# A cross-attention and mixture-of-experts kernel: the loads of x behind the first pair wait for that pair, and Wq is transposed ahead of the first rows

## The chip, the cores and the metric

The kernel runs on one core of a Trainium2 chip. Its engines are TensorE (PE), VectorE (DVE), ScalarE (ACT), GpSimd (POOL) and SyncE (SP); each works through its own list of instructions in order and waits on semaphores. The metric is the device time of one execution in microseconds, as the median of several runs.

## The reference

All arrays are float32. x is 8 blocks of 128 tokens with 256 features, the context 8 blocks of 128 rows with 64.

```python
x = x + xattn(layernorm(x), ctx, Wq, Wkv, Wout)   # causal, 16 heads of 16, within each block
x = x + ffn(layernorm(x), ...)                    # 8 experts, the best 2 of a token, LoRA of rank 16

# xattn(q, latent_kv)
qp = q @ Wq.T
k, v = split(latent_kv @ Wkv.T)
attn = softmax(where(causal, qh @ kh.T * 0.25, min))
out = (attn @ vh) @ Wout.T
# ffn
logits = x @ (gate_weight + 2 * gate_lora_B @ gate_lora_A).T
weights of the top 2 of softmax(logits), divided by their sum
gup = x @ gate_up_proj[e] + 2 * lora;  h = silu(gates) * up
y = sum over the chosen e of weight * (h @ down_proj[e] + 2 * lora)
```

## The kernel before

The order of every engine is written out by hand. The 8 blocks of tokens are handled in pairs (p = 0 to 3) up to the projections, one by one in attention, and in two groups of four in the feed-forward part, where for each of 16 (group, expert) steps TensorE multiplies in float32r with split high and low parts.

The start concerns us. What happens to pair p of x:

- SP loads it into `x_sb` (line 191, semaphore `x{p}`); the four pairs are 256 KB each. Behind them stand on SP's queue the LoRA B loads (lines 194 and 195, in runs of 64 bytes), Wout (196), the LoRA A loads (199, 200), and then, for each block, the maxima of its scores (`load_max`, line 205), which are moved into rows of `q_f` before the transposed scores of that block.
- VectorE takes its statistics (`pair_stats`, lines 540 and 541), GpSimd makes rstd (`normaliser`, lines 253 and 254), VectorE normalises into `xhat` (`normalise_pair`, line 553).
- TensorE transposes xhat into a bank (`x_T`, line 833), and ScalarE copies that to `xT` (`input_copy`, line 318).
- TensorE projects: `k_proj` (line 851) needs only the context's transpose `cT` and Wkv; `q_proj` (line 804 with `wq_d`) needs `xT` and the transposed, scaled Wq. ScalarE and VectorE spread the results into `k_f` and `q_f` (lines 345 and 565).

The other inputs of the start come on ScalarE's queue (lines 320 to 324), in this order: Wkv, the first half of the context, Wq (256 KB), the second half of the context, and half of `up_w` (1 MB). GpSimd issues the other half of `up_w` (line 270) and `dn_w` (line 273) between its normalisers. Wq is transposed by four instructions (line 1109) into bank 2, and ScalarE copies them to `wq_d` (`wq_copy`, line 318).

VectorE's program begins with `pair_stats(0)`, `wkv_dup(0)`, `normalise_pair(0)`, `context_dup(0)`, `pair_stats(1)`, `k_copy(0)`, `normalise_pair(1)`, `q_copy(0)`, `wkv_dup(1)`, `context_dup(1)`, `pair_stats(2)`, `normalise_pair(2)` and then the four `max_chunk`s of block 0 (line 594). Of these, `pair_stats(1)` waits for the load of the second pair, and everything behind it in the list waits with it. TensorE transposes the maxima of block 0 (`max_T`, line 944) after its second q and k projections, and goes on to the scores of block 1.

Of the kernel before, what the change touches and what calls it, by code (L numbers as in the profile page):

```python
# [12 lines left out]
def cross_attention_moe_kernel(nc, x, ctx_kv, Wq, Wkv, Wout, gate_w, gate_A, gate_B,  # L13
# [16 lines left out]
    PN = 2 * P  # L30
# [18 lines left out]
    with ctx:  # L49
# [38 lines left out]
        first = sb("first", [P, 2])  # L88
# [99 lines left out]
        @block.sync  # L188
        def _(sp):
            for p in range(NP):  # L190
                sp.dma_start(x_sb[:, 2 * p:2 * p + 2, :], x_v[:, 2 * p:2 * p + 2, :]).then_inc(ld[f"x{p}"], 16)
            sp.wait_ge(S_("pads_zero"), 2)
            for c in range(HC):
                sp.dma_start(upB[:, c, :, 0:R], gup_B.rearrange("e (c p) r -> c p e r", p=P)[c]).then_inc(ld["upB"], 16)
                sp.dma_start(dnB[:, c, :, 0:R], down_B.rearrange("e (c p) r -> c p e r", p=P)[c]).then_inc(ld["dnB"], 16)
            sp.dma_start(wo_raw[:, :, :], Wout.rearrange("(c p) h -> p c h", p=P)).then_inc(ld["wo"], 16)
            for j in range(4):
                rows = slice(32 * j, 32 * j + R)
                sp.dma_start(upA[rows, :, :], gup_A.rearrange("(k j) r h -> j r k h", j=4)[j]).then_inc(ld["upA"], 16)
# [12 lines left out]
            for b in range(1, NT):  # L212
                load_max(b)

            for g in range(NG):

                sp.wait_ge(S_("wT_copied"), g + 1)
                sp.dma_start(w_dram[g], wT[:, g, :]).then_inc(S_("w_written"), 16)
                sp.wait_ge(S_("w_written"), 16 * (g + 1))
                for i in range(E):  # L220
                    if g == 0:
                        sp.wait_ge(S_("pv_done"), NT - 1 if i < E // 2 else NT)
                    else:
# [92 lines left out]
        def _(act):  # L316
# [30 lines left out]
            def k_copy(p):  # L347
                act.wait_ge(S_("k_proj_0"), p + 1)
                for u in range(2):
                    spread(k_f[:, 2 * u, pair(p)], K_BANK(p, 0)[:, 0:PN], u, first[:, 1 - u:2 - u], "k_by_act")  # L350

            def q_copy(p):
                act.wait_ge(S_("q_proj_0"), p + 1)
                for u in range(2):
                    spread(q_f[:, 2 * u, pair(p)], Q_BANK(p, 0)[:, 0:PN], u, zero_col[:, :], "q_by_act")

            def values(g):
                act.wait_ge(S_("v_ones"), 1)
# [70 lines left out]

            wkv_copy(0)  # L430
            context_copy(0)
            input_copy(0)
            wq_copy()
            act.wait_ge(S_("masks_made"), 1)
            k_copy(0)
            q_copy(0)
# [90 lines left out]
        def _(dve):  # L527
# [39 lines left out]
            def k_copy(p):  # L567
                dve.wait_ge(S_("k_proj_1"), p + 1)
                for u in range(2):
                    spread(k_f[:, 2 * u + 1, pair(p)], K_BANK(p, 1)[:, 0:PN], u, first[:, 1 - u:2 - u], "k_by_dve")  # L570

            def q_copy(p):
                dve.wait_ge(S_("q_proj_1"), p + 1)
                for u in range(2):
                    spread(q_f[:, 2 * u + 1, pair(p)], Q_BANK(p, 1)[:, 0:PN], u, zero_col[:, :], "q_by_dve")

            def merge(n):

# [221 lines left out]
        def _(pe):  # L800
# [14 lines left out]
            def context_T(p):  # L815
                pe.wait_ge(ld[f"ctx{p // 2}"], 16)
                if p in (1, 2):
                    pe.wait_ge(S_("k_by_dve"), 2 * p)
                if p == 3:
                    pe.wait_ge(S_("o_nat_ready"), 1)  # L820
                for t in range(2):
# [3 lines left out]
            def x_T(p):  # L825
                pe.wait_ge(S_("xhat_ready"), 2 * (p + 1))
                if p in (1, 2):
                    pe.wait_ge(S_("k_by_act"), 2 * p)
                if p == 3:
                    pe.wait_ge(S_("merged"), 6)  # L830
                for ic in range(HC):
# [22 lines left out]
            def q_proj(p):  # L854
# [1 line left out]
                if p == 0:  # L856
                    pe.wait_ge(S_("wq_ready"), 1)
                if p == 1:
                    pe.wait_ge(S_("q_by_act"), 2)
                    pe.wait_ge(S_("q_by_dve"), 2)  # L860
                if p == 2:
                    pe.wait_ge(S_("v_ready"), 2)
                    pe.wait_ge(S_("mT_copied"), 2)
# [8 lines left out]
            def v_proj(g):  # L872
                pe.wait_ge(S_("wkv_dup"), 2)
                pe.wait_ge(S_("cT_dup"), 2 * (g + 1))
                if g == 0:
                    pe.wait_ge(S_("q_by_act"), 4)
                    pe.wait_ge(S_("q_by_dve"), 4)
                    pe.wait_ge(S_("mT_copied"), 1)
                else:
                    pe.wait_ge(S_("oT_copied"), 4)  # L880
# [9 lines left out]
            def scores(s, s_js, t, t_js):  # L890

                if s is not None:
                    if s_js[0] == 0 and s % 2 == 0:
                        for by in ("q_by_act", "q_by_dve", "k_by_act", "k_by_dve"):
                            pe.wait_ge(S_(by), 2 * (s // 2 + 1))
                    for j in s_js:
                        n = NC * s + j
# [28 lines left out]
            def max_T(b):  # L926
                pe.wait_ge(S_("max_done"), NC * (b + 1))
                if b == 0:
                    pe.wait_ge(S_("q_by_act"), 4)
                if b == 1:  # L930
                    pe.wait_ge(S_("v_ready"), 2)
                if b in (2, 3):
                    pe.wait_ge(S_("merged"), 3 * (b - 2) + 2)
                if b == 4:
                    pe.wait_ge(S_("q_by_dve"), 8)
                if b == 5:
                    pe.wait_ge(S_("k_by_dve"), 8)
                if b == 6:
                    pe.wait_ge(S_("v_ready"), 4)
                if b == 7:  # L940
# [73 lines left out]
            def values(b):  # L1014
# [2 lines left out]
                if b < 2:  # L1017
                    pe.wait_ge(S_("merged"), 3 * b + 1)
                if b == 2:
                    pe.wait_ge(S_("q_by_act"), 8)  # L1020
                if b == 3:
                    pe.wait_ge(S_("k_by_act"), 8)
                if b > GT:
                    pe.wait_ge(S_("merged"), 2 * b - 3)
                if b:
# [76 lines left out]
            pe.wait_ge(ld["wkv"], 16)  # L1102
            wkv_T(0)
            context_T(0)
            x_T(0)
            pe.wait_ge(ld["wq"], 16)
            for ic in range(HC):
                for oc in range(HC):
                    last = pe.transpose(bank[2][:, ic * H + oc * P:ic * H + (oc + 1) * P],
                                        wq_raw[:, oc, ic * P:(ic + 1) * P], ident[:, :])  # L1110
            last.then_inc(S_("wq_T"), 1)
            k_proj(0)
            q_proj(0)
            wkv_T(1)
# [14 lines left out]
            for b in range(NT):  # L1129
# [8 lines left out]
                if b == 1:  # L1138
# [1 line left out]
                    pe.wait_ge(S_("merged"), 3)  # L1140
                    pe.transpose(bank[7][0:R, 0:E], gb_raw[:, :], ident[0:E, 0:E]).then_inc(S_("gb_T"), 1)
                    pe.wait_ge(ld["wo"], 16)
                    pe.wait_ge(S_("k_by_dve"), 6)
                    for ic in range(HC):
                        for oc in range(HC):
                            last = pe.transpose(bank[5][:, ic * H + oc * P:ic * H + (oc + 1) * P],
# [19 lines left out]
                if b == 0:  # L1166
                    pe.wait_ge(ld["upA"], 64)
                    pe.wait_ge(ld["dnA"], 64)
                    pe.wait_ge(S_("k_by_act"), 6)
                    pe.wait_ge(S_("q_by_act"), 6)  # L1170
                    pe.wait_ge(S_("q_by_dve"), 6)
                    lora_products(range(3))
                if b == 1:
                    pe.wait_ge(S_("oT_copied"), 1)
# [77 lines left out]
```

## Time and profile before

| | us |
|---|---|
| median of 3 runs | 166.98 (166.35 to 167.42) |
| the profiled execution | 165.62 |
| its span | 163.9 |

| engine | busy us | share of the span |
|---|---|---|
| TensorE | 151.0 | 92% |
| VectorE | 105.4 | 64% |
| ScalarE | 80.1 | 49% |
| GpSimd | 53.7 | 33% |

The span runs from the first to the last instruction that the profiler records; the execution's own time is 1.72 us more. The page's chain is followed back from the last instruction: at each step to what released it. Transfers are busy in two stretches early on (the inputs, up to 24 us) and later around the expert weights of the tokens and the stores.

### The profile page before, as it was taken

To read this page: it belongs to the slowest core of one execution; us is meant where nothing else is said; L and a number is where in the kernel's file an instruction comes from. 1 tells how busy PE (TensorE), PEld (TensorE's weight loads), DVE (VectorE), ACT (ScalarE), POOL (GpSimd) and SP (SyncE) were. 2 spreads that over 40 slices of the span, in tenths; PEclk is the share of its full clock that TensorE was granted. 3 is DMA by queue.
4 is the path that set the end of the run, shared out by engine and by line. 5 is a ranking of instruction groups with operands and counts; after the bars stand their busy time and mean duration, and the time that the engine had idled before them with its cause. 6 is when DMAs were issued, how large, how long until landed. Compare 5 with 4: busy or idle time off the path is not lost.

```text
span 163.9 us, 3777 instructions
## 1 busy us (share of the span) xinstructions
PE 151.0 (92%) x1481; PEld 119.7 (73%) x1481; DVE 105.4 (64%) x224; ACT 80.1 (49%) x161; POOL 53.7 (33%) x93
## 2 busy tenths in 40 slices
PE   0598599999999999999999999999999999999991
PEld 0275366676786677777887887888888888888991
DVE  2757887695957664884459835884696348744443
ACT  1364247654675757766676452664463222222230
POOL 5271401245638575777773124351000000000000
PEclk9999999999999999999999999999999999999999
DMA  5999960000000000000000017600000873000003
GB/s 130 308 263 200 258 213 0 2 7 5 4 4 1 3 6 4 2 4 2 4 0 0 4 42 244 231 4 0 2 0 15 224 278 130 0 0 0 4 0 128
DMA packets 13041, 11.18 MB, mean 68 GB/s; under 512 B 6456, under 2 KB 10448, under 8 KB 13024
## 3 DMA queue, kind: packets, MB, share of 16 engines
q1 hardware_dynamic: 9584, 7.14, 16.4%
q0 software_dynamic: 544, 2.10, 4.5%
q10 hardware_dynamic: 2896, 1.70, 4.1%
q8 instruction: 12, 0.20, 0.5%
q14 instruction: 5, 0.04, 0.1%
HBM read 9.79 MB, written 1.08 MB: 66 GB/s over the span
## 4 chain that ended last, share of the span: by engine, by line
PE 77%; DVE 13%; issue 2%; DMA 2%; ACT 2%; POOL 1%; DVEq 0%; ACTq 0%
PE bank L804 37%; PE bank L1093 11%; PE bank L914 7%; DVE m_sb L594 4%; PE bank L1030 4%; PE bank L900 4%; PE bank L921 3%; DMA x_sb<-in_x 2%; PE bank L979 2%; DVE xhat L553 2%; PE bank L1011 1%; PE bank L833 1%; PE bank L885 1%; PE bank L990 1%; DVE up_w L587 1%
## 5 line engine op out<-in xcount | busy, mean ns | idle before, releaser
L295 POOL TENSOR_SCALAR_AFFINE_SELECT probsT<-probsT 128x512 f32<-128x512 f32 x32 | 19.8, 638 | 21.3 <-ACT probsT L391 21.3
L391 ACT ACTIVATE probsT<-bank 128x512 f32<-128x512 f32 x32 | 18.0, 590 | 17.3 <-PE bank L921 17.3
L804 PE MATMUL bank<-xT_hi,up_hi 128*128 128x512 f32 x64 | 26.1, 407 | 0.0
L594 DVE TENSOR_REDUCE m_sb<-bank 128x4 f32<-128x512 f32 x32 | 20.4, 683 | 8.7 <-PE bank L914 8.7
L804 PE MATMUL bank<-xT_hi,up_lo 128*128 128x512 f32 x64 | 25.3, 395 | 0.0
L804 PE MATMUL bank<-xT_lo,up_hi 128*128 128x512 f32 x64 | 25.3, 395 | 0.0
L318 ACT ACTIVATE h_hi<-h_f 128x512 fp32r<-128x512 f32 x16 | 10.1, 631 | 29.9 <-PE bank L1093 24.9
L677 DVE TENSOR_TENSOR h_lo<-h_f,h_hi 128x512 fp32r<-128x512 f32 x16 | 12.5, 780 | 10.1 <-ACT h_hi L318 10.1
L921 PE MATMUL bank<-q_f,k_f 32*128 32x128 f32 x256 | 18.6, 283 | 0.0
L1093 PE MATMUL bank<-dn_hi,h_hi 128*128 128x256 f32 x64 | 18.2, 285 | 0.1
L1093 PE MATMUL bank<-dn_hi,h_lo 128*128 128x256 f32 x64 | 17.9, 279 | 0.0
L1093 PE MATMUL bank<-dn_lo,h_hi 128*128 128x256 f32 x64 | 17.8, 279 | 0.0
L914 PEld LDWEIGHTS bank<-k_f,q_f 32*128 32x128 f32 x256 | 13.6, 186 | 5.5 <-issue 5.5
L914 PE MATMUL bank<-k_f,q_f 32*128 32x128 f32 x256 | 16.3, 283 | 0.0
L921 PEld LDWEIGHTS bank<-q_f,k_f 32*128 32x128 f32 x256 | 15.5, 186 | 0.7 <-issue 0.7
L672 DVE TENSOR_TENSOR h_f<-probsT,gated 128x512 f32<-128x512 f32 x16 | 11.1, 696 | 6.2 <-DMA probsT<-weights 5.9
L804 PEld LDWEIGHTS bank<-xT_hi,up_lo 128*128 128x128 f32 x64 | 12.0, 188 | 2.9
L804 PEld LDWEIGHTS bank<-xT_hi,up_hi 128*128 128x128 f32 x64 | 12.0, 188 | 2.2
L804 PEld LDWEIGHTS bank<-xT_lo,up_hi 128*128 128x128 f32 x64 | 12.0, 188 | 2.2
L286 POOL TENSOR_TENSOR up_lo<-up_w,up_hi 128x512 fp32r<-128x512 f32 x8 | 10.2, 1277 | 9.8 <-ACT up_hi L318 9.8
L665 DVE TENSOR_TENSOR gated<-bank,silu 128x512 f32<-128x512 f32 x16 | 11.0, 688 | 3.2 <-issue 2.1
L1093 PEld LDWEIGHTS bank<-dn_hi,h_hi 128*128 128x128 f32 x64 | 12.0, 187 | 0.9 <-DVE h_lo L677 0.3
(137 smaller groups left out, 284.8 us busy)
## 6 DMA issues: line engine op xcount, KB each, us to landing
probsT<-weights SPq DMA_DIRECT2D x16, 256.0 KB, 5.3
x_sb<-in_x SPq DMA_DIRECT2D x4, 256.0 KB, 4.4
up_w<-in_L_ffn_gate_up_proj ACTq DMA_DIRECT2D x1, 1024.0 KB, 10.3
up_w<-in_L_ffn_gate_up_proj POOLq DMA_DIRECT2D x1, 1024.0 KB, 7.4
dn_w<-in_L_ffn_down_proj POOLq DMA_DIRECT2D x1, 1024.0 KB, 7.1
out<-x_sb SPq DMA_DIRECT2D x4, 256.0 KB, 2.2
ctx_sb<-in_ctx ACTq DMA_DIRECT2D x2, 128.0 KB, 5.6
wq_raw<-in_L_xattn_Wq ACTq DMA_DIRECT2D x1, 256.0 KB, 5.5
```

Of the source, the lines that this page charges most:

```text
L286: pool.tensor_tensor(merge_slice(up_lo, dn_lo, n), merge_slice(up_w, dn_w, n), merge_slice(up_hi, dn_hi, n).bitcast(F32), ALU.subtract).th ...
L295: pool.affine_select(out=ch, in_=ch, compare_op=ALU.is_ge, fill=0.0, base=0, pattern=[[0, 4], [1, P]], channel_multiplier=-1).then_inc(S_( ...
L318: act.activation(out_, in_, ACT.Copy, scale=scale).then_inc(S_(done), 1)
L391: act.activation(probsT[:, b % 2, 4 * j:4 * j + 4, :].rearrange("p h n -> p (h n)"), bank[2 + j % 2][:, :], ACT.Exp).then_inc(S_("exp_done ...
L594: dve.reduce_max(m_sb[:, b % 2, :].rearrange("p (u j t) -> p j u t", u=2, t=2)[:, c], S_BANK(b, c)[:, :].rearrange("p (u t n) -> p u t n", ...
L665: dve.tensor_tensor(gated[:, k, :], bank[2 + k][:, :], silu[:, k, :], ALU.mult).then_inc(S_("gated_ready"), 1)
L672: dve.tensor_tensor(h_f[:, k, :], weight_all[:, n % E, :], gated[:, k, :], ALU.mult).then_inc(S_("h_ready"), 1)
L677: dve.tensor_tensor(h_lo[:, k, :], h_f[:, k, :], h_hi[:, k, :].bitcast(F32), ALU.subtract)\
L804: last = pe.matmul(out_, a, m, start=start and i == 0, stop=stop and i == len(pairs) - 1, **kw)
L914: last = pe.matmul(S_BANK(s, j)[:, c * P:(c + 1) * P], q_f[rows, c, tokens(s)], k_f[rows, c, tokens(s)], start=False, stop=True, skip_grou ...
L921: last = pe.matmul(bank[2 + j % 2][:, c * P:(c + 1) * P], k_f[rows, c, tokens(t)], q_f[rows, c, tokens(t)], start=True, stop=True)
L1093: last = pe.matmul(bank[6 + t // 2][:, (t % 2) * H:(t % 2 + 1) * H], a[:, k, tok], w[:, e, :], start=i == 0 and t % 2 == 0 and m == 0, sto ...
```

## The change

SP issues the first pair of x as before, and then waits until it has landed before it issues the other three; the rest of its queue follows. On TensorE the wait for Wq and its four transposes stand ahead of the four transposes of the first pair's xhat, and ScalarE's two copies are exchanged in the same way. In addition four semaphores are renamed (`k_by_act` to `k_copied_0`, `k_by_dve` to `k_copied_1`, and the same for q), with no effect on what waits for what. The line numbers of what follows move by one or two.

```diff
@@ sync queue @@
             for p in range(NP):
+                if p == 1:
+                    sp.wait_ge(ld["x0"], 16)
                 sp.dma_start(x_sb[:, 2 * p:2 * p + 2, :], x_v[:, 2 * p:2 * p + 2, :]).then_inc(ld[f"x{p}"], 16)
             sp.wait_ge(S_("pads_zero"), 2)
@@ ScalarE, start of its program @@
             wkv_copy(0)
             context_copy(0)
+            wq_copy()
             input_copy(0)
-            wq_copy()
             act.wait_ge(S_("masks_made"), 1)
             k_copy(0)
@@ TensorE, start of its program @@
             wkv_T(0)
             context_T(0)
-            x_T(0)
             pe.wait_ge(ld["wq"], 16)
             for ic in range(HC):
                 for oc in range(HC):
                     last = pe.transpose(bank[2][:, ic * H + oc * P:ic * H + (oc + 1) * P],
                                         wq_raw[:, oc, ic * P:(ic + 1) * P], ident[:, :])
             last.then_inc(S_("wq_T"), 1)
+            x_T(0)
             k_proj(0)
             q_proj(0)
```

On TensorE, at the start of its program, before (the tile written, then the tiles read; x4 is four in a row; `wq_raw` is Wq as loaded):

```order
L812 MATMUL bank<-ident,wkv_raw 64x128 x2
L822 MATMUL bank<-ident,ctx_sb 64x128 x2
L833 MATMUL bank<-ident,xhat 128x128 x4
L1109 MATMUL bank<-ident,wq_raw 128x128 x4
L851 MATMUL bank<-cT,wkv_d 128x256 x2
L804 MATMUL bank<-xT,wq_d 128x256 x4
L812 MATMUL bank<-ident,wkv_raw 64x128 x2
```

And with the change:

```order
L814 MATMUL bank<-ident,wkv_raw 64x128 x2
L824 MATMUL bank<-ident,ctx_sb 64x128 x2
L1110 MATMUL bank<-ident,wq_raw 128x128 x4
L835 MATMUL bank<-ident,xhat 128x128 x4
L853 MATMUL bank<-cT,wkv_d 128x256 x2
L806 MATMUL bank<-xT,wq_d 128x256 x4
L814 MATMUL bank<-ident,wkv_raw 64x128 x2
```

The four transposes of Wq have moved ahead of the four that read xhat, directly behind those of the context; what follows is in the same order. On ScalarE, behind its five DMA issues and the load of its table, before:

```order
L318 ACTIVATE wkv_d<-bank 64x256
L318 ACTIVATE cT<-bank 64x256
L318 ACTIVATE xT<-bank 128x512
L318 ACTIVATE wq_d<-bank 128x512
L345 ACTIVATE k_f<-bank,first,mine 128x256 x2
L345 ACTIVATE q_f<-bank,zero_col,mine 128x256 x2
```

And with the change:

```order
L320 ACTIVATE wkv_d<-bank 64x256
L320 ACTIVATE cT<-bank 64x256
L320 ACTIVATE wq_d<-bank 128x512
L320 ACTIVATE xT<-bank 128x512
L347 ACTIVATE k_f<-bank,first,mine 128x256 x2
L347 ACTIVATE q_f<-bank,zero_col,mine 128x256 x2
```

The copy to `wq_d` stands ahead of the copy to `xT`. On SP, whose waits are shown in brackets, before:

```order
L191 DMA x_sb<-in_x 128x2x256 x4
L194 DMA upB<-in_L_ffn_gup_lora_B 128x8x16 [waits pads_zero]
L195 DMA dnB<-in_L_ffn_down_lora_B 128x8x16
L194 DMA upB<-in_L_ffn_gup_lora_B 128x8x16
L195 DMA dnB<-in_L_ffn_down_lora_B 128x8x16
```

And with the change:

```order
L193 DMA x_sb<-in_x 128x2x256
L193 DMA x_sb<-in_x 128x2x256 [waits ld_x0]
L193 DMA x_sb<-in_x 128x2x256 x2
L196 DMA upB<-in_L_ffn_gup_lora_B 128x8x16 [waits pads_zero]
L197 DMA dnB<-in_L_ffn_down_lora_B 128x8x16
L196 DMA upB<-in_L_ffn_gup_lora_B 128x8x16
```

The second load of x now waits for the semaphore of the first, and what stands behind it in the list comes after that wait.

## Rows read from the trace of the kernel before

**Rows 1.** The page: busy us (share of the span) xinstructions; then the chain's shares.
```profile
PE 151.0 (92%) x1481; PEld 119.7 (73%) x1481; DVE 105.4 (64%) x224; ACT 80.1 (49%) x161; POOL 53.7 (33%) x93
...
PE 77%; DVE 13%; issue 2%; DMA 2%; ACT 2%; POOL 1%; DVEq 0%; ACTq 0%
```

**Rows 2.** Chain of waits, 0 to 33 us: start us, us, what.
```profile
0.79 3.29 DMA x_sb<-in_x
...
6.59 0.75 DVE xhat L553 x2
...
7.38 1.11 PE bank L833 x4
8.49 0.85 PE bank L1109 x4
9.35 1.16 PE bank L851 x4
10.50 2.09 PE bank L804 x8
...
17.95 2.40 DVE m_sb L594 x4
```

**Rows 3.** Timeline of TensorE: start us, us, engine, instructions [idle before <-releaser].
```profile
5.88 0.64 PE L822 MATMUL bank<-ident,ctx_sb 128*64 128x128 f32 x2 [0.65 <-DMA ctx_sb<-in_ctx]
...
12.65 0.60 PE L833 MATMUL bank<-ident,xhat 128*128 128x128 f32 x4
...
20.39 0.28 PE L944 MATMUL bank<-ident,m_sb 128*16 128x128 f32 x1 [1.71 <-DVE m_sb L594]
...
25.90 0.38 PE L921 MATMUL bank<-q_f,k_f 32*128 32x128 f32 x2
```

**Rows 4.** Timeline of VectorE, 4 to 18 us.
```profile
7.36 0.29 DVE L562 COPY cT<-cT 64x256 f32<-64x256 f32 x1
7.68 0.43 DVE L540 BATCH_NORM_STATS2 stats<-x_sb 128x6 f32<-128x256 f32 x1
...
10.58 0.99 DVE L565 TENSOR_SCALAR k_f<-bank,mine,first 128x256 f32<-128x256 f32 x2 [1.73 <-PE bank L851]
11.49 1.00 DVE L553 TENSOR_SCALAR xhat<-x_sb,mv,rstd 128x256 f32<-128x256 f32 x2
```

**Rows 5.** Timeline of GpSimd, 2 to 18 us.
```profile
9.25 0.72 POOL L254 TENSOR_TENSOR rstd<-var_eps,minus_half 128x2 f32<-128x2 f32 x1
...
16.92 0.93 POOL L273 DMA_DIRECT2D dn_w<-in_L_ffn_down_proj  x1
```

**Rows 6.** Timeline of ScalarE and its DMA issues, 0 to 14 us.
```profile
1.87 0.53 ACTq L322 DMA_DIRECT2D wq_raw<-in_L_xattn_Wq  x1
...
8.53 0.60 ACT L318 ACTIVATE xT<-bank 128x512 f32<-128x512 f32 x1 [1.60 <-PE bank L833]
```

**Rows 7.** Tile x_sb, 0 to 26 us: issues (ns min/median/max, first and last start), time to landing.
```profile
L191 SPq DMA_DIRECT2D x_sb<-in_x x4: 433/458/472, 0.8 to 2.3; - x4
...
DMA to landing us min/median/max: 3.3/4.4/6.2
```

**Rows 8.** DMA issues: queue, KB each, us to landing.
```profile
dn_w<-in_L_ffn_down_proj POOLq DMA_DIRECT2D x1, 1024.0 KB, 7.1
out<-x_sb SPq DMA_DIRECT2D x4, 256.0 KB, 2.2
...
wq_raw<-in_L_xattn_Wq ACTq DMA_DIRECT2D x1, 256.0 KB, 5.5
wo_raw<-in_L_xattn_Wout SPq DMA_DIRECT2D x1, 256.0 KB, 7.8
```

**Rows 9.** Windows: span, engines busy (xinstructions), granted clock, DMA share, GB/s.
```profile
7.40:10.80 3.40, 3.40 (x13) 2.42 (x14) 1.57 (x6) 1.40 (x3) 1.63 (x4) 1.00 1.25 262
```

**Rows 10.** Timeline of SP's issues, 11 to 75 us.
```profile
16.22 0.42 SPq L200 DMA_DIRECT2D dnA<-in_L_ffn_down_lora_A  x1
21.00 1.26 SPq L205 DMA_DIRECT2D q_f<-mT  x2
```

More of the change, by code:

```diff
@@ L349, in k_copy @@
                 for u in range(2):
-                    spread(k_f[:, 2 * u, pair(p)], K_BANK(p, 0)[:, 0:PN], u, first[:, 1 - u:2 - u], "k_by_act")
+                    spread(k_f[:, 2 * u, pair(p)], K_BANK(p, 0)[:, 0:PN], u, first[:, 1 - u:2 - u], "k_copied_0")
             def q_copy(p):
@@ L354, in q_copy @@
                 for u in range(2):
-                    spread(q_f[:, 2 * u, pair(p)], Q_BANK(p, 0)[:, 0:PN], u, zero_col[:, :], "q_by_act")
+                    spread(q_f[:, 2 * u, pair(p)], Q_BANK(p, 0)[:, 0:PN], u, zero_col[:, :], "q_copied_0")
             def values(g):
@@ L569, in k_copy @@
                 for u in range(2):
-                    spread(k_f[:, 2 * u + 1, pair(p)], K_BANK(p, 1)[:, 0:PN], u, first[:, 1 - u:2 - u], "k_by_dve")
+                    spread(k_f[:, 2 * u + 1, pair(p)], K_BANK(p, 1)[:, 0:PN], u, first[:, 1 - u:2 - u], "k_copied_1")
             def q_copy(p):
@@ L574, in q_copy @@
                 for u in range(2):
-                    spread(q_f[:, 2 * u + 1, pair(p)], Q_BANK(p, 1)[:, 0:PN], u, zero_col[:, :], "q_by_dve")
+                    spread(q_f[:, 2 * u + 1, pair(p)], Q_BANK(p, 1)[:, 0:PN], u, zero_col[:, :], "q_copied_1")
             def merge(n):
@@ L817, in context_T @@
                 if p in (1, 2):
-                    pe.wait_ge(S_("k_by_dve"), 2 * p)
+                    pe.wait_ge(S_("k_copied_1"), 2 * p)
                 if p == 3:
@@ L827, in x_T @@
                 if p in (1, 2):
-                    pe.wait_ge(S_("k_by_act"), 2 * p)
+                    pe.wait_ge(S_("k_copied_0"), 2 * p)
                 if p == 3:
@@ L858, in q_proj @@
                 if p == 1:
-                    pe.wait_ge(S_("q_by_act"), 2)
-                    pe.wait_ge(S_("q_by_dve"), 2)
+                    pe.wait_ge(S_("q_copied_0"), 2)
+                    pe.wait_ge(S_("q_copied_1"), 2)
                 if p == 2:
@@ L875, in v_proj @@
                 if g == 0:
-                    pe.wait_ge(S_("q_by_act"), 4)
-                    pe.wait_ge(S_("q_by_dve"), 4)
+                    pe.wait_ge(S_("q_copied_0"), 4)
+                    pe.wait_ge(S_("q_copied_1"), 4)
                     pe.wait_ge(S_("mT_copied"), 1)
@@ L893, in scores @@
                     if s_js[0] == 0 and s % 2 == 0:
-                        for by in ("q_by_act", "q_by_dve", "k_by_act", "k_by_dve"):
+                        for by in ("q_copied_0", "q_copied_1", "k_copied_0", "k_copied_1"):
                             pe.wait_ge(S_(by), 2 * (s // 2 + 1))
@@ L928, in max_T @@
                 if b == 0:
-                    pe.wait_ge(S_("q_by_act"), 4)
+                    pe.wait_ge(S_("q_copied_0"), 4)
                 if b == 1:
@@ L934, in max_T @@
                 if b == 4:
-                    pe.wait_ge(S_("q_by_dve"), 8)
+                    pe.wait_ge(S_("q_copied_1"), 8)
                 if b == 5:
-                    pe.wait_ge(S_("k_by_dve"), 8)
+                    pe.wait_ge(S_("k_copied_1"), 8)
                 if b == 6:
@@ L1019, in values @@
                 if b == 2:
-                    pe.wait_ge(S_("q_by_act"), 8)
+                    pe.wait_ge(S_("q_copied_0"), 8)
                 if b == 3:
-                    pe.wait_ge(S_("k_by_act"), 8)
+                    pe.wait_ge(S_("k_copied_0"), 8)
                 if b > GT:
@@ L1142, in _ @@
                     pe.wait_ge(ld["wo"], 16)
-                    pe.wait_ge(S_("k_by_dve"), 6)
+                    pe.wait_ge(S_("k_copied_1"), 6)
                     for ic in range(HC):
@@ L1168, in _ @@
                     pe.wait_ge(ld["dnA"], 64)
-                    pe.wait_ge(S_("k_by_act"), 6)
-                    pe.wait_ge(S_("q_by_act"), 6)
-                    pe.wait_ge(S_("q_by_dve"), 6)
+                    pe.wait_ge(S_("k_copied_0"), 6)
+                    pe.wait_ge(S_("q_copied_0"), 6)
+                    pe.wait_ge(S_("q_copied_1"), 6)
                     lora_products(range(3))
```

## The prediction

> **What bounds the kernel now.** I read four views in this order. The page's busy shares and its chain come first [rows 1]: TensorE is busy for 92% of the span and makes 77% of the chain that ended last, VectorE another 13%. So the end moves when TensorE's work starts sooner or later, or when a gap in it opens or closes. The change touches only the start, so the second view is the chain in order of time there [rows 2]. The reader should see five links: the first pair of x lands at 0.79 + 3.29 = 4.08 us; statistics and normalising end at 7.34 (6.59 + 0.75); then TensorE runs without a break through four transposes of xhat (1.11), four of Wq (0.85), the k projection (1.16) and the q projection (2.09); VectorE's chain follows down to the first maxima, 17.95 to 20.35; and TensorE is released at 20.39 after 1.71 idle [rows 3]. From there it is nearly always busy. The third view is each engine's timeline beside this path [rows 3 to 6], for what is queued behind what. The fourth is the landing of transfers [rows 7, 8].
>
> The point that matters: the four transposes of Wq stand on the path between xhat and the k projection, though they need nothing from xhat. Before 7.38 TensorE has been waiting: its context transposes end at 5.88 + 0.64 = 6.52 and xhat comes 0.86 later. Wq itself was issued at 1.87 and took 5.5 [rows 6, 8], so it landed at about 7.37, exactly when xhat was ready. In the order of before it cost nothing that Wq came so late; moved forward alone, it would find its tile only at 7.37.
>
> **Part 1: Wq ahead of the first rows.** Nothing is added: four transposes and one ScalarE copy (0.60) trade places with four transposes of xhat and their copy (0.60). If Wq is in by 6.5, its transposes run from about 6.55. They took 0.85 in the chain; started alone, as those of xhat at 7.38 were, the four need up to 1.11 to the end of the last, so they are over at 7.4 to 7.7, and TensorE's input side is free at 7.4. The xhat transposes go at 7.38 as before, and end at 8.49. ScalarE copies Wq before 8.3 and xT at 8.53 as before [rows 6], done at 9.13. The k projection needs nothing more than the copies of cT (VectorE, 7.36 + 0.29 [rows 4]) and so starts 0.85 sooner, at 8.5. The q projection follows 1.16 later, at 9.65, by when xT (9.13) is there: also 0.85 sooner. VectorE's k copy moves from 10.58 to 9.73 and ends at 10.72, and the normalising of the second pair, which stands behind it in VectorE's queue, goes from 11.49 to 10.64 if its rstd is there; rstd was ready at 9.25 + 0.72 = 9.97 [rows 5]. So 0.85 reaches the second xT, the q copies, the third pair and the first maxima. **Gain 0.85.**
>
> The bounds of this term: the transposes here run slowly. Four of xhat take 1.11 at 7.38 and 0.60 at 12.65 [rows 2, 3], a ratio of 1.85, although the granted clock is given as 1.00 in this stretch too [rows 9]; I read the durations as the lower of the two clock levels until shortly after 10.5, and the upper one after. If TensorE speeds up at the same instant as before (about 10.8) while the q projection starts 0.85 sooner, then 0.85 of it runs slowly that did not: a loss of 0.85 x (1 - 1/1.85) = 0.39, and 0.46 is left. If it speeds up sooner, the gain grows (first rival). I take 0.85, since the busy stretch that came before the rise starts sooner by about as much.
>
> **Part 2: the loads held.** x1, x2 and x3 no longer stand behind x0 in SP's queue from 0.8 to 2.3, but are issued from about 4.15. Three things follow.
> - x0 itself: did the later pairs slow it? The four were issued 0.5 apart and took from 3.3 (the first) to 6.2 (the last) [rows 7], that is they landed from 4.08 to about 8.5, 1.5 apart on average: one after another, not together. So x0 was hardly shared with x1, and I take 0. The upper bound is the store of the same 256 KB at the end, 2.2 with little else moving [rows 8]: 1.1 less. The lower bound is 0; one transfer less ahead of or beside x0 can't delay it.
> - ScalarE's queue has the engines to itself from about 3.5 to 5.2. Traffic runs at 262 GB/s from 7.4 to 10.8 [rows 9]; I take that rate for the stretch before too, which x1 and x2 shared. At their spacing of 1.5 some 256 KB or more of them moved between x0's landing and Wq's last bytes; at 262 GB/s that is 1.0 us of transfer. So ctx0 (5.88 before [rows 3]) should land about 0.6 sooner and Wq about 1 us sooner, at 6.1 to 6.5. Bounds: 7.37 (nothing gained) down to 4.1 (2.2 after its issue, as the store). What it costs if this fails: with Wq at 7.37, its transposes run first, those of xhat 0.85 later, and the k projection starts at 9.35 as before; xT is copied by 9.98, still before 10.50. So part 1 then gains nothing and loses nothing.
> - x1 is late. Its statistics started at 7.68 behind the cT copy that ended at 7.65 [rows 4], so it had 2.4 us to spare. Issued at 4.15 it lands at 7.45 with x0's 3.3 (the nearest row: same size, same queue, empty before it), at 6.35 with the store's 2.2, and at 10.35 with x3's 6.2. I take 7.45: no cost. The slack beyond it: from the start of statistics to rstd is 9.97 - 7.68 = 2.29, and normalising can start at 10.64, so x1 may land as late as 8.25 before any of the 0.85 is lost, and up to 9.1 before the kernel is slower than it was.
>
> The Trainium skill (DMA: Bandwidth & Descriptors, Two DMAs through the same engine are not ordered) says that descriptors of one queue on one engine start in order. By that rule, the trace agrees: holding x1 buys x0 nothing, and speaks against the hold as a help for x0. The same page (Anatomy of one DMA) gives a fit of 2.0 us plus bytes over 436 GB/s, measured on another issuing path; an estimate by it puts x1 at 4.15 + 2.6 = 6.75, and the sum would not change.
>
> **What queues behind the held loads.** SP issues the small LoRA loads, Wout, the LoRA A loads and then the maxima of the first block behind the x loads, some 2 us later at first. Their first readers on TensorE come after 24 us, and none of the landings named in the rows is later than 24.0 (dn_w: 16.92 + 7.1 [rows 5, 8]). The tightest is the maxima: issued at 21.00 [rows 10], read by the transposed scores at 25.90 [rows 3]. They will be issued at 20.15 and read at 25.05; SP's last load before them was issued by 16.64 [rows 10], so 2 us of delay there fit. Taken at 0. The bound is Wout's 7.8 [rows 8]: with it they land at 27.95, 2.9 late.
>
> **Sum.** The profiled execution took 165.62 (span 163.9 and 1.72 around it). 165.62 - 0.85 + 0 + 0 = 164.77. The median of the three runs shown is 1.36 above that execution; by medians the forecast is 166.98 - 0.85 = **166.1**. After 20.39 I find nothing that would give the gain back: what TensorE waits for later is VectorE and ScalarE, which shift with it.
>
> **Rivals.**
> 1. TensorE speeds up earlier (chance 0.15). Wq's transposes fill the time before 7.38, so TensorE works nearly without a break from about 5. If the xhat transposes run at 0.60 instead of 1.11 and the k projection at 1.16/1.85 = 0.63, another 1.04 is there; but rstd of the second pair (9.97) caps it: normalising can go from 11.49 to 10.0 at best, so 1.49 in all, and 165.5. For it: the same instruction is 1.85 times faster once TensorE has been busy. Against: only transposes are added before 7.38. The Trainium skill (TensorE: Matmul & The Clock Gate, Part 4: PE-mode transpose) holds that transposes don't count as activity for the clock; no row here shows it, and by it this rival would not come about.
> 2. x0 sooner (0.05): up to 1.1 on top of 0.85, but SP, VectorE and GpSimd then wait for Wq or for x1; I price it at half, 165.6 to 165.0.
> 3. Nothing moves (0.09): Wq lands no earlier than 7.37, because the traffic of ScalarE's own queue, not x, sets it. 167.0.
> 4. Slower (0.09): x1 is late. One mechanism: SP's held loads come back into full traffic (ctx1 and 1 MB of up_w already queued by ScalarE) and take x3's 6.2 or even Wout's 7.8. VectorE waits at the statistics of the second pair, with the k copy behind them. Landing at 10.35 costs 10.35 - 9.1 = 1.25: 168.2; landing at 11.95 costs 2.85: 169.8. It decides from 9.1 on. Against: x0's own 3.3 was reached with ScalarE's queue beside it.
>
> **How the numbers follow.** The likeliest case has 0.62 and 166.1, its own range 165.4 to 166.8 from its bounds of 0.46 and about 1.2 and the spread of the runs shown (166.35 to 167.42). With rivals 1 to 3 and a part of 4 the range that should hold 8 in 10 is 164.9 to 167.3. About 1%, 1.67 us, is what a measurement of this kernel can tell from no change. Faster than 165.3: a part of rival 1, most of 2 and the edge of the first case, 0.20. Slower than 168.65: the later half of rival 4 and the unforeseen, 0.06. Within 1%: 0.74.
>
> **What would show it.** In the new profile: x0 still lands at 4.0 to 4.1; Wq's transposes start before 6.8 and end before xhat's start at 7.4; the k projection starts near 8.5, normalising of the second pair near 10.6, the first maxima near 17.0; and TensorE's release by the maxima's transpose falls at about 19.5. x1's landing shows in whether VectorE sits idle before 7.7's statistics. The prediction is wrong if that wait ends after 8.3, if Wq's transposes still start at 7.4, or if the xhat transposes take 0.6 instead of 1.1.

## The result, and the profile after

| | before | after |
|---|---|---|
| median, us | 166.66 (6 runs, 165.65 to 167.51) | 168.50 (6 runs, 168.03 to 169.19) |
| the profiled execution | 165.62 | 168.08 |
| its span | 163.9 | 166.3 |

The changed kernel takes 1.0115 times as long, 95% interval 1.0084 to 1.0147: 1.8 us slower, where 0.85 less was forecast. (The ratio is estimated from all single times; it is not the quotient of the two medians, which in this document differs from it by up to 0.0024.) It came out by rival 4, x1 late, to which I had given 0.09.

The page's busy line and its chain, which answer [rows 1]:

```profile
PE 153.4 (92%) x1470; PEld 121.4 (73%) x1481; DVE 105.6 (63%) x224; ACT 80.0 (48%) x161; POOL 53.3 (32%) x93
...
PE 72%; DVE 14%; DMA 6%; issue 3%; ACT 2%; POOL 1%; DVEq 0%; ACTq 0%
```

TensorE has lost share of the chain, and transfers have gone from 2% to 6%. The chain of waits at the start (start us, us, what) says which one, against [rows 2]:

```profile
0.79 3.21 DMA x_sb<-in_x
...
4.02 7.23 DMA x_sb<-in_x
...
20.39 2.40 DVE m_sb L596 x4
...
22.83 0.28 PE bank L946
```

The load of the second pair now stands on the path for 7.23 us, where it didn't appear before. The four transposes of Wq and the k projection have left the chain. TensorE's timeline shows that this part went as forecast, up to the q projection:

```profile
6.00 1.11 PE L1110 MATMUL bank<-ident,wq_raw 128*128 128x128 f32 x4 [0.28 <-DMA wq_raw<-in_L_xattn_Wq]
...
7.23 1.11 PE L835 MATMUL bank<-ident,xhat 128*128 128x128 f32 x4
...
8.27 1.23 PE L853 MATMUL bank<-cT,wkv_d 64*128 64x256 f32 x4
...
9.43 3.78 PE L806 MATMUL bank<-xT,wq_d 128*128 128x256 f32 x8
...
15.04 0.66 PE L835 MATMUL bank<-ident,xhat 128*128 128x128 f32 x4 [1.62 <-DVE xhat L555]
```

Wq's transposes start at 6.00, those of xhat at 7.23, the k projection at 8.27. Then the second xhat transposes wait 1.62 for VectorE, and the maxima's transpose comes at 22.83 instead of 20.39 [rows 3]: 2.44 later, as much as the span is longer. VectorE's timeline has the reason, against [rows 4]:

```profile
11.28 0.43 DVE L542 BATCH_NORM_STATS2 stats<-x_sb 128x6 f32<-128x256 f32 x1 [3.79 <-DMA x_sb<-in_x]
...
12.37 0.96 DVE L567 TENSOR_SCALAR k_f<-bank,mine,first 128x256 f32<-128x256 f32 x2
13.61 1.38 DVE L555 TENSOR_SCALAR xhat<-x_sb,mv,rstd 128x256 f32<-128x256 f32 x2 [0.28 <-POOL rstd L256]
```

It sits idle for 3.79 us at the statistics of the second pair, with the k copy behind them. SP issued the three held loads at once when x0 was in, 4.02 to 5.63, and the tile's landings say 7.2 for x1 (the least of the three; the 3.2 is x0's) and 7.9 for the last:

```profile
L193 SPq DMA_DIRECT2D x_sb<-in_x x4: 379/450/667, 0.8 to 5.2; - x4
...
DMA to landing us min/median/max: 3.2/7.4/7.9
```

Why so long? The queues' traffic from 4 to 8 us, first before, then after (queue: packets, MB, share of 16 engines; q1 is SP's, q10 ScalarE's):

```profile
q1 hardware_dynamic: 1059, 0.71, 63.6%
q10 hardware_dynamic: 1328, 0.55, 53.0%
```

```profile
q10 hardware_dynamic: 1802, 1.24, 107.3%
```

Before, the two queues shared the engines. After, SP's queue has no row in that stretch: it moved nothing from 4.02, when the first of the held loads was issued, to 8. From 8 to 11 it moves 0.77 MB:

```profile
q1 hardware_dynamic: 1081, 0.77, 86.0%
```

So x1 was not slowed by sharing; it had to wait until ScalarE's queue, with the second half of the context and 1 MB of up_w already in it, had nearly run out: 1.24 MB of it went from 4 to 8, and the last 0.25 MB beside SP's loads from 8 to 11. The rates show that no bandwidth was missing, 311 GB/s from 4 to 8 (314 before), and one more thing (span, engines busy, granted clock, DMA share, GB/s):

```profile
4.00:8.00 4.00, 2.97 (x12) 1.79 (x12) 2.44 (x8) 2.15 (x4) 0.95 (x2) 1.00 1.07 311
...
16.00:20.00 4.00, 3.75 (x37) 2.31 (x38) 2.33 (x8) 0.59 (x2) 1.70 (x4) 0.57 0.86 255
```

TensorE's granted clock was 0.57 on average from 16 to 20, that is mostly the lower of its two levels, after TensorE had been idle for the most part from 13.4 to 15.0. Before it was 1.00 there.

### The profile page after: what moved, and what is told of

It reads as the page before. It is cut to its first block, busy times and chain, and to the rows that moved or that the text cites. A ratio compares the mean times of both kernels' runs of the same rounds, so it can differ in the third digit from the quotient of the medians.

```text
span 166.3 us, 3766 instructions
## 1 busy us (share of the span) xinstructions
PE 153.4 (92%) x1470; PEld 121.4 (73%) x1481; DVE 105.6 (63%) x224; ACT 80.0 (48%) x161; POOL 53.3 (32%) x93
## 4 chain that ended last, share of the span: by engine, by line
PE 72%; DVE 14%; DMA 6%; issue 3%; ACT 2%; POOL 1%; DVEq 0%; ACTq 0%
PE bank L806 36%; PE bank L1095 11%; PE bank L916 7%; DMA x_sb<-in_x 6%; DVE m_sb L596 4%; PE bank L1032 4%; PE bank L923 3%; PE bank L902 3%; DVE xhat L555 2%; PE bank L981 2%; PE bank L1013 1%; PE bank L887 1%; PE bank L992 1%; DVE up_w L589 1%; DVE stats L542 1%
## 5 line engine op out<-in xcount | busy, mean ns | idle before, releaser
L916 PEld LDWEIGHTS bank<-k_f,q_f 32*128 32x128 f32 x256 | 14.4, 203 | 5.9 <-issue 5.9
L916 PE MATMUL bank<-k_f,q_f 32*128 32x128 f32 x256 | 17.2, 302 | 0.0
```

The costliest lines, as they stand in the source:

```text
L916: last = pe.matmul(S_BANK(s, j)[:, c * P:(c + 1) * P], q_f[rows, c, tokens(s)], k_f[rows, c, tokens(s)], start=False, stop=True, skip_grou ...
```

## The experiments

Theory H: the held loads are served only when ScalarE's backlog is through, and VectorE's wait for x1 is the whole loss. Rival S: the new order on TensorE costs by itself. Rival C: the lower clock is a good part of the loss. Ratios are against the kernel before on the same chip, and the three values in the column "before" are three chips. Each kernel ran 12 times, but "hold from x2, spare transposes" only 6 times at first, and the ratios of "hold only" and "TensorE kept busy" rest on 9 times each.

| kernel | median, us | before | ratio (95%) |
|---|---|---|---|
| exchange only | 167.01 | 166.34 | 1.0045 (1.0015 to 1.0075) |
| hold only | 168.14 | 166.34 | 1.0097 (1.0062 to 1.0132) |
| both, up_w late | 165.85 | 166.34 | 0.9950 (0.9921 to 0.9980) |
| both, hold from x2 | 165.74 | 166.34 | 0.9952 (0.9928 to 0.9976) |
| both, TensorE kept busy | 168.22 | 166.91 | 1.0085 (1.0051 to 1.0119) |
| hold from x2, no exchange | 166.54 | 166.91 | 0.9986 (0.9959 to 1.0013) |
| exchange, Wq on SP's queue | 165.97 | 166.91 | 0.9940 (0.9912 to 0.9967) |
| hold from x2, spare transposes | 165.21 | 166.91 | 0.9885 (0.9844 to 0.9926) |
| the same again | 166.05 | 166.59 | 0.9948 (0.9916 to 0.9980) |
| hold from x2, again | 166.15 | 166.59 | 0.9957 (0.9927 to 0.9988) |
| hold from x2, spare products | 165.91 | 166.59 | 0.9935 (0.9898 to 0.9972) |
| Wq on SP's queue, spare products | 165.44 | 166.59 | 0.9925 (0.9890 to 0.9960) |

### Each part alone

Exchange only: the change without these two lines.

```diff
-                if p == 1:
-                    sp.wait_ge(ld["x0"], 16)
```

> Only the exchange of the Wq transposes with the xhat transposes; the four x loads are issued in a row as before. Theory H (the held loads are served only when ScalarE's backlog is through, and VectorE's wait for x1 is the whole loss): x1 lands at 5.3 as before, VectorE has no wait at the statistics of the second pair, Wq lands at about 7.4, its transposes start at 7.4 and the exchange moves nothing: 166.7, within 0.5. Rival S (the new order itself costs, by the wait for Wq ahead of the xhat transposes, or through TensorE's clock): 167.5 to 168.5.

It was 0.45% slower, which neither theory had said: less than S, and not H's nothing. Its times fall in two groups, seven from 166.34 to 167.09 and five from 167.92 to 168.26, and the profiled one, at 167.98, is of the slower five. TensorE's timeline shows why that one was slow:

```profile
7.21 0.63 PE L822 MATMUL bank<-ident,ctx_sb 128*64 128x128 f32 x2 [1.85 <-DMA ctx_sb<-in_ctx]
8.83 1.11 PE L1108 MATMUL bank<-ident,wq_raw 128*128 128x128 f32 x4 [0.98 <-DMA wq_raw<-in_L_xattn_Wq]
9.73 1.06 PE L833 MATMUL bank<-ident,xhat 128*128 128x128 f32 x4
10.72 1.23 PE L851 MATMUL bank<-cT,wkv_d 64*128 64x256 f32 x4
```

In this execution the context came at 7.21 and Wq at 8.83, 1.4 later than in the profile of before. VectorE had made xhat by 7.45 (6.71 + 0.74), and its transposes stood behind Wq's until 9.73; the k projection started at 10.72, 1.44 later than before. As an estimate from these rows, 0.99 of it (from 9.73 to 10.72) is the order's, since the old one would have had the xhat transposes done while it waited for Wq; the other 0.45 is the late Wq's own. So the order is not free of risk: it puts whatever Wq is late by on the path of xhat. That a late Wq is what sets the other four slow executions apart is likely, but only one was profiled.

Hold only: the two lines alone, in the kernel before.

```diff
+                if p == 1:
+                    sp.wait_ge(ld["x0"], 16)
```

> Only the hold; TensorE and ScalarE keep the order of before. H: x1 lands at about 11.2, the second pair's normalising starts at about 13.6, time 168.5 within 0.5, the same as with both parts, since the k projection 0.85 earlier buys nothing while VectorE waits. S: 166.7, since without the exchange there is no loss.

Ratio 1.0097, on H's side, and against S; the 1.0115 of both parts can't be told from it, as the intervals overlap. VectorE's row for the second pair's statistics, and the maxima's transpose on TensorE:

```profile
10.45 0.43 DVE L542 BATCH_NORM_STATS2 stats<-x_sb 128x6 f32<-128x256 f32 x1 [3.09 <-DMA x_sb<-in_x]
```

```profile
22.00 0.28 PE L946 MATMUL bank<-ident,m_sb 128*16 128x128 f32 x1 [1.89 <-DVE m_sb L596]
```

x1 lands 0.8 earlier here than with both parts and the maxima's transpose comes 0.8 earlier too: 22.00 against 22.83, and 20.39 before.

### Is it ScalarE's backlog?

Both parts of the change, and up_w issued later:

```diff
-            act.dma_start(up_w[:, 0, :, :], gate_up.rearrange("e (c p) o -> c p e o", p=P)[0]).then_inc(ld["up0"], 16)
...
             k_copy(0)
             q_copy(0)
+            act.dma_start(up_w[:, 0, :, :], gate_up.rearrange("e (c p) o -> c p e o", p=P)[0]).then_inc(ld["up0"], 16)
             wkv_copy(1)
```

> Both parts of the change, and ScalarE issues its 1 MB of up_w behind its first q copies (about 12.6) instead of at 2.95. H: x1 finds ScalarE's queue empty once the second half of the context is through (about 6.3) and lands at 7.0 to 7.8; the statistics start at 7.7, and part 1's 0.85 shows at last: 165.8 (165.3 to 166.3). If the long latency of x1 is not made by that backlog, x1 still lands after 10 and the time stays at 168.5. S: 168 or more.

165.85, as H said: taking 1 MB out of ScalarE's queue turned 1.0115 into 0.9950, 0.8 us less than before by the ratio (0.5 by the two medians). VectorE's statistics of the second pair and its normalising:

```profile
8.37 0.43 DVE L542 BATCH_NORM_STATS2 stats<-x_sb 128x6 f32<-128x256 f32 x1 [0.91 <-DMA x_sb<-in_x]
...
10.69 1.38 DVE L555 TENSOR_SCALAR xhat<-x_sb,mv,rstd 128x256 f32<-128x256 f32 x2 [0.16 <-POOL rstd L256]
```

x1 was in at 8.3, not at the 7.0 to 7.8 expected: ScalarE's queue still had the second half of the context to move, and SP's queue moved nothing from 4 to 5, its first 0.09 MB from 5 to 6 beside ScalarE's last 0.13 MB, and had the engines alone from 6 to 7 (0.28 MB). 8.3 is just the 8.25 up to which the prediction had found slack. In this execution the gain did not get through. TensorE's q projection and its transpose of the maxima:

```profile
9.39 3.18 PE L806 MATMUL bank<-xT,wq_d 128*128 128x256 f32 x8
...
20.36 0.28 PE L946 MATMUL bank<-ident,m_sb 128*16 128x128 f32 x1 [1.71 <-DVE m_sb L596]
```

The q projection took 3.18 instead of the 2.16 of the profile before, and the maxima's transpose came at 20.36 against 20.39. The section on why the prediction was wrong compares it with executions of the same pace. SP's queue moved 0.59 MB from 4 to 8:

```profile
q1 hardware_dynamic: 679, 0.59, 56.6%
q10 hardware_dynamic: 835, 0.38, 35.2%
```

Both parts, but the hold one pair later:

```diff
-                if p == 1:
+                if p == 2:
                     sp.wait_ge(ld["x0"], 16)
```

> Both parts, but x1 is issued right behind x0 and only x2 and x3 wait for x0. H: x1 lands by 5.3, x2 at about 11.3 (needed at 13.6), Wq at 6.5 to 7.0, xhat transposes start at 7.3, k projection at 8.5: 165.9 (165.4 to 166.5). S: 168 or more.

0.9952, and 0.9957 when it was measured again on another chip. With x1 issued ahead, the steps come as the prediction had worked them out:

```profile
6.66 1.11 PE L1110 MATMUL bank<-ident,wq_raw 128*128 128x128 f32 x4 [0.20 <-DMA wq_raw<-in_L_xattn_Wq]
7.56 1.06 PE L835 MATMUL bank<-ident,xhat 128*128 128x128 f32 x4
8.55 1.08 PE L853 MATMUL bank<-cT,wkv_d 64*128 64x256 f32 x4
...
19.43 0.28 PE L946 MATMUL bank<-ident,m_sb 128*16 128x128 f32 x1 [1.79 <-DVE m_sb L596]
19.54 1.84 PE L902 MATMUL bank<-causal,ident_b 128*128 128x512 bf16 x4
```

```profile
7.56 0.43 DVE L542 BATCH_NORM_STATS2 stats<-x_sb 128x6 f32<-128x256 f32 x1
...
10.63 0.96 DVE L555 TENSOR_SCALAR xhat<-x_sb,mv,rstd 128x256 f32<-128x256 f32 x2
```

The k projection starts at 8.55 and the second normalising at 10.63 (8.5 and 10.64 were forecast). The maxima's transpose is 0.96 earlier than before, and 0.8 (0.7 in the repeat) is what the ratio says over 12 runs (0.6 and 0.4 by the medians). The profiled execution itself did not keep it: behind the maxima's transpose the causal products took 1.84 instead of the 1.03 that they take at the upper clock, and its span is 164.8; the last part of this section comes back to that. x2 and x3 landed up to 7.6 after their issue, and nobody needed them by then.

Hold from x2 without the exchange, that is the kernel before with two lines:

```diff
             for p in range(NP):
+                if p == 2:
+                    sp.wait_ge(ld["x0"], 16)
```

> Only x2 and x3 wait for x0, and TensorE and ScalarE keep the order of before. If the exchange is what pays in the version with both (0.5% below the kernel before): no difference to the kernel before (within 0.3%), k projection at 9.3. If the calmer transfers alone pay: 0.5% below it.

0.9986, no difference within the interval, and its k projection starts at 9.40 instead of 8.55: the calmer transfers alone give no gain clear of the noise. By the times alone the two versions are hardly told apart (0.9959 to 1.0013 here, 0.9928 to 0.9976 with the exchange); that the exchange is what pays, once Wq comes early, rests on the traces beside them.

The exchange with Wq moved to SP's queue:

```diff
-                if p == 1:
-                    sp.wait_ge(ld["x0"], 16)
                 sp.dma_start(x_sb[:, 2 * p:2 * p + 2, :], x_v[:, 2 * p:2 * p + 2, :]).then_inc(ld[f"x{p}"], 16)
+                if p == 0:
+                    sp.dma_start(wq_raw[:, :, :], Wq.rearrange("(c p) h -> p c h", p=P)).then_inc(ld["wq"], 16)
```

> The exchange without the hold, and Wq is loaded on SP's queue right behind x0 instead of third on ScalarE's. Theory H with what the first four runs showed (the exchange pays when Wq is in before xhat and x1 before 8.3): Wq lands at about 5.4, x1 at about 6.7, Wq's transposes start by 6.0, k projection at 8.5: 165.6 beside 166.3 for the kernel before (0.4% less). If a queue that is third in line is served in bursts here too, x1 may land after 8.3 and the gain shrinks to nothing.

0.9940, 0.6% less where 0.4% was expected, with the k projection at 8.57. Its profiled execution, like that of the version with up_w late, had a slow q projection (2.94) and the maxima's transpose at 20.46. Wq on SP's queue without the exchange was not run. No wait is needed to bring Wq forward; its place in a queue does it.

### Does the clock matter?

The changed kernel, with spare work where TensorE sat idle:

```diff
             wkv_T(1)
+            for _ in range(14):
+                pe.transpose(bank[2][:, 0:P], ident[:, :], ident[:, :])
             x_T(1)
```

> Both parts of the change, and 14 spare transposes of the identity into a free bank between the second Wkv transposes and the second xhat transposes, where TensorE sat idle from 13.4 to 15.0 and then ran at a granted clock of 0.50 from 17 to 19. They compute nothing that is used. Theory H (VectorE's wait for x1 is the loss): the granted clock stays at 1.00 there, scores of block 0 take 1.17 instead of 2.09, but the first maxima still come at 20.3, since VectorE's chain sets them: no change against the changed kernel, 168.1 to 168.5 beside a kernel before at 166.3 to 166.7. Rival C (the lower clock is a good part of the loss): 0.9 or more is won back, 167.4 or less.

TensorE's rows, of the spare work, the scores of block 0 and the maxima's transpose:

```profile
12.37 1.69 PE L1118 MATMUL bank<-ident 128*128 128x128 f32 x14
...
17.33 1.17 PE L916 MATMUL bank<-k_f,q_f 32*128 32x128 f32 x32
...
22.97 0.28 PE L946 MATMUL bank<-ident,m_sb 128*16 128x128 f32 x1 [1.91 <-DVE m_sb L596]
```

The scores take 1.17, not the 2.09 that they took in the profile after, so the clock stayed up; and the maxima's transpose comes at 22.97 against 22.83: nothing won on the path, as H said. The ratio (1.0085) is lower than the changed kernel's 1.0115 and the intervals overlap. The 0.9 us that rival C wanted would be a ratio of 1.006 or less, near the end of the interval; so by the times alone C is unlikely, and a smaller share for the clock stays possible.

Spare transposes ahead of everything, in the version that holds from x2:

```diff
             pe.wait_ge(S_("ident_made"), 1)
+            def spare(n):
+                for _ in range(n):
+                    pe.transpose(bank[2][:, 0:P], ident[:, :], ident[:, :])
+            spare(10)
             pe.wait_ge(ld["wkv"], 16)
             wkv_T(0)
+            spare(3)
             context_T(0)
```

> The version that holds only x2 and x3, with 10 spare transposes of the identity before the first Wkv transposes and 3 between them and the context's, so that TensorE works from 2.1 on. They compute nothing that is used. If transposes alone raise TensorE's clock: those of xhat take 0.6 instead of 1.06, the k projection 0.7 instead of 1.08, normalising of the second pair starts at 10.0 instead of 10.63: 0.5 less than that version, 0.8% below the kernel before (165.0). If they don't: the same time as that version, 0.5% below the kernel before (165.6).

> The version with 13 spare transposes again. If spare transposes do nothing (its profile showed the slow pace up to 10.7, as without them): equal to the version without them in the same call, within 0.3. If its lower time in the last call (1.15% below the kernel before, from 6 runs) was real: 0.5 below that version.

The first time it was 1.15% below the kernel before from only 6 runs, the second time 0.52% from 12, beside 0.43% without the spare work on the same chip: no difference that the ratios show. The two times were on two chips. The profiles of the two differ more than the times. TensorE's rows of the first run: the xhat transposes, the maxima's transpose, the scores of block 1:

```profile
7.54 1.06 PE L835 MATMUL bank<-ident,xhat 128*128 128x128 f32 x4
...
20.02 0.28 PE L946 MATMUL bank<-ident,m_sb 128*16 128x128 f32 x1 [1.71 <-DVE m_sb L596]
...
21.09 1.17 PE L916 MATMUL bank<-k_f,q_f 32*128 32x128 f32 x32
```

And of the second, with Wq's transposes first, and then its window from 20 to 24 (granted clock third from the end):

```profile
6.68 0.66 PE L1116 MATMUL bank<-ident,wq_raw 128*128 128x128 f32 x4 [0.41 <-DMA wq_raw<-in_L_xattn_Wq]
7.29 0.65 PE L835 MATMUL bank<-ident,xhat 128*128 128x128 f32 x4
...
19.14 0.28 PE L946 MATMUL bank<-ident,m_sb 128*16 128x128 f32 x1 [1.90 <-DVE m_sb L596]
```

```profile
20.85 2.09 PE L916 MATMUL bank<-k_f,q_f 32*128 32x128 f32 x32
```

```profile
20.00:24.00 4.00, 4.00 (x43) 2.73 (x43) 1.94 (x4) 1.05 (x3) 0.00 (x0) 0.63 0.76 230
```

The same program went slowly through the xhat transposes in one execution (1.06) and fast in the other (0.65), on another chip. In the fast one the maxima's transpose came at 19.14, 0.9 sooner than in the slow one; but there TensorE had been idle for 1.90 before it, and from 20 to 24 the granted clock was 0.63 on average. The scores of block 1 took 2.09 instead of 1.17, and the lead was given back. The idle time alone does not settle it: the clock stayed at 1.00 from 20 to 24 behind an idle time of 1.71 (first run), and in the profile of both parts with TensorE kept busy it was up at the same place behind 1.91. And it fell to 0.62 and 0.66 in both profiles of the version that holds from x2, without spare work and with slow xhat transposes, behind 1.79 and 1.90. What decides it is open.

Beside it, on the same chip, stood products in place of the transposes (5 and 2), in the version that holds from x2 and in that with Wq on SP's queue, and the version without spare work:

```diff
-                    pe.transpose(bank[2][:, 0:P], ident[:, :], ident[:, :])
+                    pe.matmul(bank[2][:, 0:P], ident[:, :], ident[:, :], start=True, stop=True)
```

> The version that holds only x2 and x3, with spare float32 products of the identity with itself (5 before the first Wkv transposes, 2 behind them) in place of the 13 spare transposes, about the same time on TensorE. Nothing of them is used. In the run with spare transposes TensorE was busy from 2.1 on and the transposes of xhat still went at the slow pace (1.06 for four). If products raise the clock where transposes don't: xhat's four take 0.6 or the k projection 0.7, normalising of the second pair starts at 10.0 to 10.3, time 0.3 to 0.8 below the unwarmed version of the same call. If they don't either: no difference to it beyond 0.3.

> The exchange with Wq on SP's queue behind x0 and no hold, with the same spare products. If they raise the clock: below the version that holds x2 and x3 by what the clock gives, 0.8 to 1.2% below the kernel before. If not: 0.6% below it, as without them.

> The version that holds only x2 and x3, unchanged, again, so that the versions with spare work are compared with it on one chip in one call: 0.5% below the kernel before.

0.9935, and 0.9925 with Wq on SP's queue; not separable from 0.9957 and 0.9940. Both profiles look like the second one above, with the same price behind it; that of the version that holds from x2:

```profile
7.23 0.66 PE L835 MATMUL bank<-ident,xhat 128*128 128x128 f32 x4
...
19.08 0.28 PE L946 MATMUL bank<-ident,m_sb 128*16 128x128 f32 x1 [1.89 <-DVE m_sb L596]
...
20.15 2.02 PE L916 MATMUL bank<-k_f,q_f 32*128 32x128 f32 x32
```

The exchange with Wq on SP's queue and the spare products has the lowest ratio of what was timed 12 times, 0.9925; what it has over the plain one (0.9940) is within the noise.

These two medians hide something. With spare products the 12 times fall in two groups with a gap of over 1 us between them, and the median lies at the edge of one or in the gap:

| kernel | lower group, us | upper group, us |
|---|---|---|
| hold from x2, spare products | 5 of 12, 164.40 to 164.60 | 7 of 12, 165.88 to 166.45 |
| Wq on SP's queue, spare products | 6 of 12, 164.48 to 164.90 | 6 of 12, 165.97 to 166.24 |

Both profiled executions (165.88 and 165.97) are of the upper group, and they are the ones that lost the clock between 20 and 24 (granted 0.57 and 0.61). Over the whole execution the granted clock of the first kernel's lower group was 0.996 to 0.998, that of its upper group 0.986 to 0.990; in the second kernel four of the upper six have 0.985 to 0.990 and two have 1.00, so there the clock is not the whole story. The likely reading is that an early clock was kept in about half of the executions and was then worth 2 us against the kernel before (164.5 against 166.59), of which the exchange has 0.7 by the ratio; no execution of a lower group was profiled, so this is not shown.

## Why the prediction was wrong

**The step that failed** is "x1 is late": "I take 7.45: no cost", the latency of x0 taken for a load issued 3.3 later. I chose the nearest row by size and queue, and gave 0.09 to the case in which SP's load comes back into ScalarE's full queue. The latency was 7.2, nearer to Wout's 7.8 [rows 8], which was the row to take: a 256 KB load that SP issued at 11.78, 0.59 behind GpSimd's issue of 1 MB of up_w. In the profile after, the same load of Wout was issued at 13.20, ahead of that megabyte (14.79), and took 3.6. I had even written that x0's 3.3 was reached "with ScalarE's queue beside it"; but both queues began together then, and neither had a backlog. The runs with up_w later and with x1 ahead of the hold each take this one cost away, and both give a gain, so the cause is shown.

**Its price was right.** I had put the point from which it costs at 9.1 for x1. (Its own sum, 11.49 - 2.29, gives 9.20, and 8.35 where it says 8.25; the 0.1 changes nothing.) It landed at 11.25, so 2.15 later, and the second normalising came 2.12 later (13.61 against 11.49). It also took 1.38 instead of 1.00, beside GpSimd's work on the causal mask, and the maxima's transpose was 2.44 later. The median moved by 1.84: less than those 2.44, which are counted from a profile before that had a fast q projection, and more than the 1.48 by which 22.83 lies behind the old order with a slow one (21.35, see the next paragraph).

**Part 1 was right up to the start of the q projection**: Wq's transposes from 6.00 to 7.1, xhat's at 7.23, the k projection at 8.27, which is 1.0 earlier than before. Whether its 0.85 then reaches the maxima has to be read between executions whose q projection went at the same pace. At the fast one (2.0 to 2.2) the maxima's transpose is at 20.39 in the old order and at 19.43 and 19.30 in the new (hold from x2, both times). At the slow one (2.9 to 3.2) it is at 21.35 in the old order (hold from x2, no exchange) and at 20.36 and 20.46 in the new (up_w late, Wq on SP's queue). That is 0.9 to 1.1 each time. The profile before happened to be one at the fast pace, at 165.62 under a median of 166.66, and so it flatters the kernel before. By the ratios the three versions in which x1 is in time are 0.50, 0.48 and 0.60% faster than before, 0.8 to 1.0 us (0.7 in the repeat; 0.4 to 0.9 by the medians), near the 0.85. What was wrong in it is that alone it "gains nothing and loses nothing": it lost 0.45%, for which its profile shows one reason, a Wq that came 1.4 later.

**x0 unhurried was right**: 3.21 against 3.29. Holding x1 bought x0 next to nothing.

**The clock** (rival 1): with Wq's transposes ahead of them, those of xhat still took 1.11 in the profile after. The q projection even took 3.78 against 2.16, starting sooner in the slow stretch, more than the 0.39 that I had allowed. Here it was hidden behind VectorE's wait. In the second run with spare transposes TensorE had done nothing but transposes when those of Wq and xhat went at the fast pace (0.66 and 0.65); in the first it had done the same and they went slowly. The rule of the Trainium skill (TensorE: Matmul & The Clock Gate, Part 4: PE-mode transpose), that transposes don't count as activity for the clock, doesn't fit the second of these executions. What decides between the two is open: they were on two chips, and on the second chip the version without spare work went slowly there (1.11 and 1.06) and all three with spare work fast; one profile of each is too few to say more.

**What stays open:** why ScalarE's queue shut SP's out instead of sharing as before. The traces show it wherever SP issued a load into a backlog, in all nine profiles that have the hold and up_w in its old place: SP's queue moves nothing from 5 to 8. Service in the order of issue across the queues would fit them, and Wout's 7.8 and 3.6 too; how the engines choose between queues was not tested by itself. The Trainium skill (DMA: Bandwidth & Descriptors, Queues, rings and completion order) has each engine go round between the queues it has work for, packet by packet; 4 us without a row for SP's queue in the profile after don't agree with that, and the measurement decides.

## What to carry to other kernels

A load that is held back doesn't come back to the place it had: it went behind what the other queue had put in meanwhile (7.2 us instead of 3.9 for x1 issued behind x0). Before holding one, ask who waits for it first, and take its latency from a row of a load that was issued into a backlog, not from the first load of the kernel. To bring a load forward, move it in its queue (Wq behind x0) or hold only what nobody needs soon, and keep the megabyte that nobody needs yet out of the other queue. Moving work ahead on an engine pays only as far as its own input is early in every execution; otherwise its wait is passed on to what was moved behind it. And look at the single times before trusting a median: where they fall in two groups, the one profiled execution belongs to one of them.

## What the runs showed of the hardware

- A queue can be shut out entirely: no row for SP's queue from 4 to 8 while ScalarE's moved 1.24 MB at 311 GB/s, with three loads of SP issued from 4.02 on (profile after). In the kernel before, with both queues filled from the start, they moved 0.71 and 0.55 MB in the same 4 us.
- TensorE's clock rose at very different times in two executions of one program: four xhat transposes took 1.06 and 0.65 with the same work before them, on two chips. In all three profiles where it was up early it fell again behind 1.9 us of idle time, with 0.57 to 0.63 granted from 20 to 24 and 2.02 to 2.09 instead of 1.17 for the scores. But 1.89 and 1.91 of idle time at the same place left it at 1.00 in two other kernels (hold only, TensorE kept busy).
- The same load of 256 KB (Wout) took 7.8 us when SP issued it 0.59 behind GpSimd's 1 MB, and 3.6 when it was issued 1.59 ahead of it.
